# Side rows of the distances as high and low halves in one 128-row fp32r matmul, the last batch's query operands on GpSimd, and a new instruction order

## The reference

```python
xn = layernorm(x)
x = x + linear_attention(xn, 16 heads of 64) + moe(xn)      # 64 experts of width 88, top 8 of the rows' scores, and shared ones
xn = layernorm(x)
x = x + window_attention(xn) + ternary_ffn(xn)              # on batches of 512 rows
```

```python
q, v = relu(xn @ enc_q), relu(xn @ enc_v)                   # 8 heads x 16
m = softplus(base + 0.1 * mlp(mean(q)))                     # a weight for each of the 128 columns
dist = sqrt(sum(m * (q[k] - q[t])**2) + 1e-8)               # k in the window of t
w = exp(-dist) of the 32 nearest, normalised
out = (q * (w @ v + gate * 0.1 * hebb(q))) @ decoder
```

## Time and profile before

| | us |
|---|---|
| median of 3 runs | 739.52 (737.44 to 740.01) |
| the profiled execution: its time | 739.74 |
| its span, first to last instruction | 737.9 |
| PE busy | 667.7 (90%) |
| DVE busy | 596.5 (81%) |
| ACT busy | 414.0 (56%) |
| POOL busy | 367.5 (50%) |

### The profile page before, as it was taken

The page is one execution under the profiler, slowest core; times in us unless marked ns, Lnnn a source line. Parts: engine busy times, 40 slices in busy tenths (PEclk is TensorE's granted clock), DMA queues, the critical chain, the costliest instruction groups (busy, mean ns, idle before and its releaser), DMA issues.

```text
span 737.9 us, 12696 instructions
## 1 busy us (share of the span) xinstructions
PE 667.7 (90%) x3984; PEld 443.9 (60%) x3984; DVE 596.5 (81%) x2527; ACT 414.0 (56%) x759; POOL 367.5 (50%) x406
## 2 busy tenths in 40 slices
PE   3899999999999999999899999999999999889722
PEld 2555676666556666666556676666666566677621
DVE  3888657987986999899938999948759999549983
ACT  2555245467566847466557575454877463478600
POOL 2157255656553766456535955646634666222220
PEclk9999999999999999999998999999999999999955
DMA  9930000000000000000000000000100000010101
GB/s 288 365 95 1 0 1 0 1 0 1 23 12 1 10 11 18 8 13 17 17 1 1 11 13 16 14 6 2 25 9 10 16 13 16 4 42 26 34 19 28
DMA packets 25727, 21.99 MB, mean 30 GB/s; under 512 B 1920, under 2 KB 23596, under 8 KB 25148
## 3 DMA queue, kind: packets, MB, share of 16 engines
q1 hardware_dynamic: 25660, 21.18, 9.6%
HBM read 18.95 MB, written 2.23 MB: 29 GB/s over the span
## 4 chain that ended last, share of the span: by engine, by line
PE 48%; DVE 37%; issue 4%; POOL 4%; ACT 3%; DMA 2%; SPq 1%; DVEq 0%; ACTq 0%; POOLq 0%
PE bank_X L512 13%; PE bank_A L512 12%; PE bank_G L512 11%; PE bank_U L512 10%; DVE S L809 9%; DVE Wk L1233 9%; DVE m L1230 6%; DVE GWk L809 2%; DMA vw<-vscratch 2%; SPq L414 1%; DVE rr L809 1%; POOL S L1550 1%; DVE hg L817 1%; DVE Wlo L809 1%; PE bank_X L521 1%
## 5 line engine op out<-in xcount | busy, mean ns | idle before, releaser
L512 PE MATMUL bank_A<-S,WdT 128*128 128x512 f32 x368 | 188.0, 613 | 2.1 <-POOL S L1550 1.2
L1550 POOL TENSOR_TENSOR Wlo<-Wgu,Whi 128x256 fp32r<-128x256 f32 x138 | 110.1, 804 | 112.9 <-ACT Whi L1293 112.7
L1550 POOL TENSOR_TENSOR S<-S,Rb 128x512 f32<-128x512 f32 x88 | 117.4, 1335 | 94.7 <-DVE S L809 94.3
L809 DVE TENSOR_TENSOR S<-S,bank_U 128x512 f32<-128x512 f32 x184 | 124.0, 679 | 43.4 <-PE bank_U L512 27.2
L1293 ACT ACTIVATE S<-bank_G 128x512 f32<-128x512 f32 x184 | 107.7, 595 | 89.5 <-PE bank_G L512 80.0
L1293 ACT ACTIVATE Whi<-Wgu 128x256 fp32r<-128x256 f32 x184 | 74.9, 414 | 93.4 <-PE bank_U L512 83.2
L512 PE MATMUL bank_U<-xH,Whi 128*128 128x512 f32 x184 | 96.2, 523 | 9.1 <-DVE S L809 8.8
L512 PE MATMUL bank_G<-xH,Whi 128*128 128x512 f32 x184 | 98.3, 534 | 3.9 <-POOL Wlo L1550 2.1
L512 PEld LDWEIGHTS bank_A<-S,WdT 128*128 128x128 f32 x368 | 66.0, 192 | 40.0 <-issue 22.3
L1233 DVE MATCH_REPLACE8 Wk<-m,Wk 128x79 f32<-128x79 f32 x384 | 82.0, 225 | 0.0
L809 DVE TENSOR_TENSOR S<-S,Rb 128x512 f32<-128x512 f32 x88 | 76.6, 874 | 2.2
(11 more groups left out here) (238 smaller groups left out, 1177.8 us busy)
## 6 DMA issues: line engine op xcount, KB each, us to landing
vw<-vscratch SPq DMA_DIRECT2D x32, 158.0 KB
Wgu<-in_Wgu SPq DMA_DIRECT2D x2, 2048.0 KB, 15.1
xs<-in_x SPq DMA_DIRECT2D x4, 256.0 KB, 6.9
wqk<-in_w_qkv SPq DMA_DIRECT2D x1, 1024.0 KB, 7.4
Wgu<-in_Wgu SPq DMA_DIRECT2D x1, 1024.0 KB, 9.0
vscratch<-mo SPq DMA_DIRECT2D x4, 256.0 KB
out<-xs SPq DMA_DIRECT2D x3, 256.0 KB, 3.0
Wgu<-in_Wgu SPq DMA_DIRECT2D x1, 512.0 KB, 5.2
```

What stands on the lines that cost most here:

```text
L512: return engine.matmul(dst, lhsT, rhs, start=start, stop=stop)
L809: return engine.tensor_tensor(dst, a, b, op)
L1550: return engine.tensor_tensor(dst, a, b, op)
```

## The change

1. **Side rows.** `La` and `Ra` become fp32r tiles of 128 rows: 64 rows for the lengths of the queries (high halves, then low ones), 16 for the keys (8 high, 8 low), 16 of mask, 32 of zeros. `nmx` grows from 136 to 272 columns, so that TensorE gives each length twice. ScalarE copies `nm` and `pq` to fp32r (that rounds: the high half); VectorE then writes value minus high into the low rows (`lengths_of_keys`, `lengths_of_queries`, one `scalar_tensor_tensor` each); ScalarE pads after that. `La` is made from the tile `PQ` in SBUF in two pieces (groups 0 and 1, then the rest), and `distances` waits for the piece. The side rows of a group are one instruction of 128 x 316 in place of two of 56 x 316.
2. **Constants.** One DMA of 128 x 444 values into `Ed[0]` replaces five into `La` and `Ra`; ScalarE copies it to fp32r in three instructions in the setup. The tile `cst`, loaded at the start, grows by 137 columns of 128 values.
3. **Queries.** In the last batch all eight spreads are GpSimd's.
4. **Orders.** All five strings are new. What they do in the last batch: on TensorE `hhffffhhffdffddffdffdtdft` becomes `hhhfffhhfdffdffddtdffdt`, where the last two `h` are `nm` and `pq`, and the first `t` after a `d` is the turn of group 0 and the last `t` its ctx. On ScalarE the head goes from `hfhhfhhfhfhhfhk` to `hfhhfhhfhhfhhhhk`: the passes of `dense` (`f`) that stood between the metric's exponential and the inverse lengths `hf` now stand behind `hf` and ahead of the metric's logarithm. The stores of the last batch all stand behind the last window load, and that of batch 2 moves from behind window 2 to behind window 4. VectorE's addition of batch 1's feed-forward moves behind seven steps of choice, and that of batch 3 to nearly the end.

```diff
     "sp":
-        "vvvvvvvvvvvvvvvvvvvvvvvvvvvvsvvsvsvvvvssvss",
+        "vvvvvvvvvvvvvvvvvvvvvvvvvvvvsvvsvvvsvvvssss",
...
-    put("pick", (np.arange(SIDE)[:, None] % NH == p[None, :] // TQ) * 1.0)
+    put("pick", (np.arange(NEAR)[:, None] % NH == p[None, :] // TQ) * 1.0)
+    put("negside", (p[:, None] // SIDE == 1) * -1.0 + ((p[:, None] >= NEAR + NH) & (p[:, None] < MASK)) * -1.0)
...
-        nmx = sb("nmx", [128, NH + 128])
-        Pk = sb("Pk", [SIDE + NH, PADK + T])
-        La = sb("La", [AUX, NG, 128])
-        Ra = [sb(f"Ra{i}", [AUX, GT, WK]) for i in range(2)]
+        nmx = sb("nmx", [128, 2 * NH + GT * NEAR])
+        Pk = sb("Pk", [MASK, PADK + T], FR)
+        PQ = sb("PQ", [NEAR, 128], FR)
+        La = sb("La", [128, NG, 128], FR)
+        Ra = [sb(f"Ra{i}", [128, GT, WK], FR) for i in range(2)]
...
         def queries_on_vector(b, g):
-            return g % 2 == 1
+            return g % 2 == 1 and b < B - 1
...
-            load("ld_e", La[SIDE:, :, :], d["extras"][SIDE:, 0:128].unsqueeze(1).to_broadcast([NH + TQ, NG, 128]))
-            for k in range(2):
-                load("ld_e", Ra[k][0:SIDE, :, :], d["extras"][0:SIDE, 128:].rearrange("p (a c) -> p a c", a=GT))
-                load("ld_e", Ra[k][SIDE + NH:, :, :],
-                     d["extras"][SIDE + NH:, 128:].rearrange("p (a c) -> p a c", a=GT))
+            load("ld_e", flat(Ed[0])[:, 0:128 + GT * WK], d["extras"])
...
-                mm(t[SIDE:SIDE + NH, :], nmx[:, 0:NH], ksq[:, :]).then_inc(sems(full(bank("nm", b))), 1)
+                mm(t[NEAR:MASK, :], nmx[:, 0:2 * NH], ksq[:, :]).then_inc(sems(full(bank("nm", b))), 1)
...
-                    pe.wait_ge(empty(bank("pq", b)), nth("pq", b) + 1)
+                    pe.wait_ge("la", 2 * b + (1 if g < 2 else 2))
                     pe.wait_ge("ra", b * NG + g + 1)
                     mm(t[:, 0:GT * WK], La[:, g, :], flat(Ra[k]), True, False)
...
+            def lengths_of_keys(b):
+                yield
+                dve.wait_ge("pk_hi", b + 1)
+                t = filled("nm", b)
+                emptied(stt(Pk[NEAR:, PADK:], Pk[NEAR:, PADK:].bitcast(F), K("negside")[NEAR:MASK, :], t[NEAR:MASK, :],
+                            ALU.mult, ALU.add), "nm", b)
+
             def lengths_of_queries(b):
                 yield
+                dve.wait_ge("pq_hi", b + 1)
                 t = filled("pq", b)
-                dve.wait_ge("ld_e", 16 * 5)
+                a = emptied(stt(PQ[:, :], PQ[:, :].bitcast(F), K("negside", NEAR), t[0:NEAR, 0:128], ALU.mult, ALU.add),
+                            "pq", b)
+                dve.wait_ge(*a)
+                dve.wait_ge("sides", 3)
                 if b > 0:
                     dve.wait_ge(full(bank("dist", b - 1, NG - 1)), nth("dist", b - 1, NG - 1) + 1)
-                q = t[0:SIDE, 0:128].rearrange("p (g t) -> p g t", g=NG).unsqueeze(2).to_broadcast([SIDE, NG, NH, TQ])
-                a = tt(La[0:SIDE, :, :].rearrange("p g (h t) -> p g h t", h=NH), q, pick4, ALU.mult)
-                emptied(a, "pq", b)
+                for g in (slice(0, 2), slice(2, NG)):
+                    n = g.stop - g.start
+                    q = PQ[:, :].bitcast(F).rearrange("p (g t) -> p g t", g=NG)[:, g, :].unsqueeze(2)
+                    tt(La[0:NEAR, g, :].rearrange("p g (h t) -> p g h t", h=NH), q.to_broadcast([NEAR, n, NH, TQ]),
+                       pick4[:, g, :, :], ALU.mult).then_inc(sems("la"), 1)
+                    yield
...
+                act(La[:, :, :], e[:, 0:128].unsqueeze(1).to_broadcast([128, NG, 128]), ACT.Copy).then_inc(sems("sides"), 1)
+                yield
+                for k in range(2):
+                    act(flat(Ra[k]), e[:, 128:], ACT.Copy).then_inc(sems("sides"), 1)
...
-                a = emptied(act(Pk[SIDE:, PADK:], t[SIDE:SIDE + NH, :], ACT.Copy), "nm", b)
-                sc_.wait_ge(*a)
-                act(Pk[SIDE:, 0:PADK], Pk[SIDE:, PADK:PADK + 1].to_broadcast([NH, PADK]), ACT.Copy).then_inc(
-                    sems("pk"), 1)
+                act(Pk[NEAR:, PADK:], t[NEAR:MASK, :], ACT.Copy).then_inc(sems("pk_hi"), 1)
+                yield
+                t = filled("pq", b)
+                if b > 0:
+                    sc_.wait_ge("la", 2 * b)
+                act(PQ[:, :], t[0:NEAR, 0:128], ACT.Copy).then_inc(sems("pq_hi"), 1)
+                yield
+                sc_.wait_ge(empty(bank("nm", b)), nth("nm", b) + 1)
+                act(Pk[NEAR:, 0:PADK], Pk[NEAR:, PADK:PADK + 1].bitcast(F).to_broadcast([2 * NH, PADK]),
+                    ACT.Copy).then_inc(sems("pk"), 1)
```

102 lines of the change are left out of this document (55 added, 47 removed).

## The result

The changed kernel takes 712.4 us (711.5 to 713.3, 4 runs) against 738.5 us (734.9 to 740.0, 4 runs) of the kernel before beside it: a ratio of 0.965, interval 0.961 to 0.969. The forecast was 726 with a range of 718.5 to 736; the gain of 26 us is nearly twice the 13.5 that I had forecast.

A forecast was written before the change was run, and what follows sets the result against it. TensorE bounds the side-row stretches, VectorE those between, window-load DMA the tail. Terms -14.4 (matmul), +3.6 (VectorE), +0.3 (constants), -3.2 (last head) sum to -13.7 from 739.5: 725.8, forecast 726, range 718.5 to 736 us.

The forecast's parts named there:

- Matmul (14.4): Side rows of batches 0 to 2: 24 steps, each 0.60 us shorter on TensorE, save 14.4 us (12.0 to 16.3).
- The few rows: Old side-row pair on TensorE: 0.1 us of each instruction goes with its 56 rows, against the skill's rule.
- VectorE in the heads and constants (3.6 + 0.3): Added VectorE work in three batches' heads costs 3.6 us (2.5 to 8); the larger constants load at the start, 0.3.
- three quarters: Share of the 4.8 us of added VectorE work in the heads of batches 0 to 2 charged as delay: 3.6 us.
- The upper bound of 8: Worst cost, in us, of VectorE's added head work, with slow La products beside GpSimd and nmx at 0.93.
- The orders themselves are a term that no row prices: New engine orders were given no size; in the bounded stretches they could only shift what waits.
- this rival: The orders bring more than the prediction's terms, giving a time below 719 us; chance 0.06.
- The end is the time of ctx of group 0 plus about 60 us, whatever the engines do: Tail: six window loads, 54 us from window 2's issue to last landing, set the end in either order; no gain.
- Last head (3.2): Last batch's head and first choice: ctx of group 0 starts 3.2 us earlier, at 675.0 not 678.25 (0 to 5).
- Moving the spreads: First choice of the last batch: two query spreads go from VectorE to GpSimd, 2.0 us less.
- La in one instruction with its successor 0.14 to 0.20 later: Confirming sign on TensorE: the side rows take one instruction, and the next starts 0.14 to 0.2 us later.
- PE still full in the stretches of the side rows: Confirming sign: TensorE stays fully busy where the side rows' matmuls of batches 0 to 2 lie.

The follow-up runs named there:

- the square: Four kernels, orders of before or new crossed with old or new side-row matmul: 737.8, 728.6, 730.7 and 712.4 us; the kernel before the change is compared beside them.
- old_orders: The changed kernel with the engine orders of before, into which only the new steps are put: 728.6 us, ratio 0.984 to the kernel before.

## Why the prediction was wrong, and where it was right

- **Matmul (14.4).** The instruction was sized right, 0.14 to 0.20 us and 0.6 saved, but the term was not: I let 24 of them come through whole. With the clock taken off 8.2 came through in the new orders and 3.8 in the old ones, where TensorE then waits for VectorE; in the one batch that needs no correction 2.7 of 4.8.
- **The few rows.** I took 0.1 us of each old instruction to go with its 56 rows, against a rule that would have made 9.4 of the 14.4. Right: with fp32 and 316 columns an instruction costs 0.36 us with 56 rows and 0.27 to 0.29 with 128. The rule was that of the Trainium skill ("TensorE: Matmul & The Clock Gate", Why this matters for your kernels), by which a single matmul with few rows takes the time of one with 128; the measurement decides against it here.
- **VectorE in the heads and constants (3.6 + 0.3).** The durations were right: low halves 0.74 and 0.34, as taken, products 0.42 to 0.94, where I had 0.82 each. `nmx`, which I let grow by 0.1, took 0.36, 1.88, 0.87 and 0.36 us in the four heads for 0.29, 0.29, 0.57 and 0.93 before; the contention with GpSimd that I had feared for the products shows in the first head alone, 1.46 for 1.29. All of it costs 2.1 by the square, and of the doubled products about 1.8 of 4.2 came through: three quarters was too much on the whole, while one head let nearly all through, as the products behind it came later. The upper bound of 8 was far off.
- **"The orders themselves are a term that no row prices; in the bounded stretches they can only shift what waits."** This is the step that failed. I had read that PE was full, 39.00 of 39.00 in the stretches of side rows, and DVE at 95 to 98% between, and concluded that either engine is at its bound in each part. But the choices of a batch and what stands beside them took 106.6 us with DVE 88% full: the two engines were full in turn, and an order can spread what each has to do, as the new ones do with the five expert steps that they put ahead of the first choices. With the clock taken off it was worth 5.2 to 10.3 us up to the last expert sum with the old form of the side rows, and 9.6 to 14.7 with the new one, and 4.2 in the one batch that needs no correction. That is not all, since the clean batch has as many expert steps as before and gained too, and moving those steps alone was not tried. I had given this rival 0.06.
- **"The end is the time of ctx of group 0 plus about 60 us, whatever the engines do", in either order.** The mechanism was right, the loads held the tail; the constant was not. The same edit that changes the sizes of tiles moves `vw` by 1604 bytes, and six loads take 5.3 us less; the stores behind the last load save about 2 more (49.2 us for six in `old_orders`, 47.1 in the changed kernel), where I had estimated 1.5 and called it unchanged.
- **Last head (3.2).** Measured 1.2. The side rows of the last batch stand 26.7 us behind the last expert sum, as before (26.4), not 0.7 earlier: the keys' matmul is waited for (ScalarE 2.12 us at 638.90), and the hand-overs follow. Behind them the turn came 3.1 us earlier (11.2 us after the side rows for 14.3, forecast 10.3) and ctx of group 0 4.75 us behind it for 3.2, as forecast. But PE was not full, as I had feared for the f steps: it waits 0.84 and 1.93 us for `Ra`, ScalarE's copy of the keys. Moving the spreads brings the turn 2.0 us forward, as forecast.
- **The clock** was no term: up to the last expert sum 10.3 us were lost before, 5.1 of them ahead of 160 us, and 1.8 after. Which edit causes it was not tried. Seen is only that the places go with the program: ahead of 160 us the ten profiles that have the orders of before up to the last expert step lose 3.4 to 5.2 us, the nine that have the new ones 0 to 1.7.
- **Signs that I had named.** La in one instruction with its successor 0.14 to 0.20 later: seen. PE still full in the stretches of the side rows: nearly, 95, 95 and 99% (220.2 to 257, 370 to 415.5 and 525 to 562.7 us), with DVE at 92, 87 and 90% where it had been at 79 to 80. DVE at 95%, which I had listed as a sign of a wrong prediction, is seen over a batch's whole choices; it was one of a gain. The side rows at 649.5: measured 641.3. SP's load of window 2 at about 665: 657.8, and the last landing 47.1 us behind it, not 54.

In sum, up to the last expert sum, for new steps, matmul, orders and clock: +2.1 - 8.2 - 5.2 - 8.5 = -19.8, or, if the clock ahead of 160 us is left out, +2.1 - 8.2 - 10.3 - 3.4, for +3.9 - 14.4 = -10.5; then -1.2 for -3.2; then -7.0 for nothing: -28.0 for -13.7. The orders, the clock and the tail brought 20.7 us that I had at nothing (how the first two divide is open, their sum of 13.7 is not); the matmul, taken 6.2 too high, hid part of the error.

What is left open: what brings the clock down at one place and not at another, and with it how much of the gain up to the last expert sum is chance; and which bits of `vw`'s place matter.

## What to carry to other kernels

When two engines are nearly full in turn, saving work on one of them is worth only what the order lets through, here 2.7 of 4.8 us in the one clean batch: price a change and a new order together, read from stretches of a whole batch how full the second engine is, and count whether work was moved out of a stretch before its times are compared. A change of one tile's size moves all tiles behind it, so a DMA that holds a tail has to be timed again, at best with a size that spreads over all engines (in the kernel before, 80 rows for 79 gave 9 us and the better place 4). And when two kernels are compared to one per cent, compare the granted clock in stretches first, from the very start of the span.
